# Loading sorted tokens one quad at a time into four smaller slots, in the last stage of a scan and routed-FFN kernel

## The reference

```python
x = x + _L0_attn_ref(_layernorm(x), ...)          # the scan
x = x + _L0_ffn_ref(_layernorm(x), ...)

def _L0_ffn_ref(x, weight, scale, expert_masks, router_w):
    logits = jnp.einsum('bsd,ed->bse', x, router_w)
    probs = jax.nn.softmax(logits, axis=-1)
    top1_w, top1_idx = jnp.max(probs, axis=-1), jnp.argmax(probs, axis=-1)
    w_q = jnp.clip(jnp.round(weight / THRESH), -1.0, 1.0)
    w_scaled = w_q * scale[:, None]
    def body(out, inputs):
        e_idx, mask_e = inputs
        y = jnp.einsum('bsi,oi->bso', x, w_scaled * mask_e)
        sel = (top1_idx == e_idx)[..., None]
        return jnp.where(sel, y * top1_w[..., None], out), None
```

## The time and the profile before

| | |
|---|---|
| time, median of 3 | 447.69 us (446.92 to 451.38) |
| span of the profiled execution | 460.4 us |
| last stage in it: first load issued, last output DMA begun | 389.62, 453.78 us |
| TensorE, VectorE, ScalarE, GpSimd busy | 64%, 84%, 39%, 63% |
| mean granted TensorE clock | 0.841 |

### The profile page before, as it was taken

One profiled execution on the slowest core, in us unless ns is written; L12 is line 12 of the kernel. 1 busy time (PEld: TensorE's weight loads), 2 busy tenths in 40 slices (PEclk: granted clock), 3 DMA queues, 4 the chain that ended last, 5 costly groups with the idle time before them and its releaser, 6 DMA issues.

```text
span 460.4 us, 4327 instructions
## 1 busy us (share of the span) xinstructions
PE 296.5 (64%) x1142; PEld 147.7 (32%) x1142; DVE 387.7 (84%) x400; ACT 180.5 (39%) x257; POOL 290.7 (63%) x135
## 2 busy tenths in 40 slices
PE   0868558756686675577666567476799213787780
PEld 0432222222232232222222233134376100666560
DVE  3999999999999999999999999999995970245441
ACT  1496545633464354354345335333033300322220
POOL 0645877568767767767767776776534485055554
PEclk9998777987887988978889888988978756689887
DMA  8006999920010010011010001000000334957400
GB/s 268 13 0 123 160 179 168 141 77 23 23 47 23 23 46 23 23 24 44 23 47 23 23 23 46 23 24 22 0 1 0 122 143 179 358 163 222 153 16 0
DMA packets 27902, 34.96 MB, mean 76 GB/s; under 512 B 3171, under 2 KB 22125, under 8 KB 27888
## 3 DMA queue, kind: packets, MB, share of 16 engines
q1 hardware_dynamic: 24000, 27.76, 26.1%
q0 software_dynamic: 2816, 6.32, 3.7%
q10 hardware_dynamic: 1072, 0.70, 0.6%
HBM read 20.03 MB, written 16.83 MB: 80 GB/s over the span
## 4 chain that ended last, share of the span: by engine, by line
DVE 43%; POOL 28%; PE 11%; issue 9%; DMA 3%; another core or an unknown queue 2%; ACT 1%; POOLq 0%; SPq 0%; DVEq 0%; ACTq 0%
DVE xs_sb L665 28%; POOL xs_sb L311 23%; PE bank L1063 5%; POOL sorted_tokens L355 4%; DVE bx L657 3%; PE bank L1004 2%; PE bank L1046 2%; DVE rows L632 2%; DMA x_sb<-in_L_attn_x_dram 2%; DVE st L573 1%; POOL out_dram L364 1%; DVE xn L594 1%; DVE wT L625 1%; DMA xs_sb<-sorted_tokens 1%
## 5 line engine op out<-in xcount | busy, mean ns | idle before, releaser
L311 POOL TENSOR_TENSOR xs_sb<-xs_sb,cb 128x1024 f32<-128x1024 f32 x64 | 208.0, 3270 | 84.6 <-DVE xs_sb L665 72.7
L665 DVE TENSOR_TENSOR_SCAN xs_sb<-dA,bx 128x1024 f32<-128x1024 f32 x64 | 199.8, 3160 | 0.0
L896 PE MATMUL bank<-xs_sb,cst 128*128 128x512 f32 x256 | 147.7, 706 | 2.0 <-POOL xs_sb L311 2.0
L444 ACT ACTIVATE cb<-bank 128x512 f32<-128x512 f32 x64 | 38.1, 596 | 146.8 <-POOL xs_sb L311 121.0
L860 PE MATMUL bank<-bc,pick 96*128 96x512 bf16 x64 | 22.7, 441 | 88.7 <-DVE bx L657 87.5
L657 DVE TENSOR_TENSOR bx<-bank,rows 128x1024 f32<-128x1024 f32 x64 | 74.5, 1203 | 0.1
L896 PEld LDWEIGHTS bank<-xs_sb,cst 128*128 128x128 f32 x256 | 55.0, 227 | 56.9 <-issue 51.7
L454 ACT ACTIVATE dA<-rows,a_neg 128x1024 f32<-128x1024 f32 x64 | 73.2, 1145 | 0.2
L364 POOL DMA_INDIRECT out_dram<-cb,to_token x32 | 31.8, 992 | 35.3 <-DVE cb L773 28.1
L548 ACT ACTIVATE xn<-bank 128x1024 f16<-128x1024 f16 x16 | 16.1, 1023 | 65.1 <-PE bank L1046 49.5
L860 PEld LDWEIGHTS bank<-bc,pick 96*128 (+1 forms) x64 | 4.0, 101 | 115.8 <-issue 79.5
(11 more groups left out here) (116 smaller groups left out, 295.0 us busy)
## 6 DMA issues: line engine op xcount, KB each, us to landing
sorted_tokens<-zero SPq DMA_DIRECT2D x1, 8224.0 KB, 55.4
mask_sb<-_L_ffn_expert_masks_dram SPq DMA_DIRECT2D x32, 256.0 KB, 2.7
xs_sb<-sorted_tokens SPq DMA_DIRECT2D x7, 1028.0 KB, 7.4
x_sb<-in_L_attn_x_dram SPq DMA_DIRECT2D x4, 512.0 KB, 7.8
xs_sb<-sorted_tokens SPq DMA_DIRECT2D x2, 514.0 KB, 3.7
out_dram<-cb,to_token POOLq DMA_INDIRECT x32
cst<-in_constants_dram ACTq DMA_DIRECT2D x1, 504.0 KB, 4.2
w_nat<-in_L_ffn_weight_dram SPq DMA_DIRECT2D x1, 256.0 KB, 9.1
```

The source lines that it names most:

```text
L311: pool.tensor_tensor(prod[:, j, dh, :], h[:, j, dh, :], cb[:, j, :], ALU.mult).then_inc(s_prod, 1)
L444: act.activation(cb[:, j, c * HC:(c + 1) * HC], c_ps, ACT.Copy).then_inc(s_cevac, 1)
L665: dve.tensor_tensor_scan(h[:, j, dh, :], dA[:, j, dh, :], bx[:, dh, :], 0.0, ALU.mult, ALU.add).then_inc(s_scan, 1)
L896: mm = pe.matmul(yacc[:, dh, c * HC:(c + 1) * HC], ident, prod[:, j, dh, c * HC:(c + 1) * HC], start=first, stop=last, skip_group_check=True)
```

## The change

`xs_sb` becomes the first 4112 numbers of each partition of the tile `h_and_prod` (which now has a name of its own; the trace of the changed kernel will call it so), with **four slots of one quad**. SP issues 16 loads of one quad, all alike; the load of quad `q` for `q >= 4` waits until quad `q - 4` has been transposed and finished. The first load's semaphore of its own goes. VectorE writes out four quads and then loops three times over a body of four. TensorE writes out four turns and multiplies and the turn of quad 4, loops twice over a body of four, and writes out the last four.

```diff
-        xs_sb = sb("xs_sb", [P, 4, 4, ROW])
-        h_and_prod = xs_sb[:, :, :, :].rearrange("p s t c -> p (s t c)")
+        h_and_prod = sb("h_and_prod", [P, 4 * DH * L])[:, :]
+        xs_sb = h_and_prod[:, 0:4 * 2 * ROW].rearrange("p (s t c) -> p s t c", s=4, t=2)
...
-            xs_v = xs.rearrange("(g t p) c -> g p t c", t=4, p=P)
+            xs_v = xs.rearrange("(q t p) c -> q p t c", t=2, p=P)
             sp.wait_ge(s_scat, 16 * TB)
-            for g in range(LOADS):
-                if g >= 4:
-                    sp.wait_ge(s_tps, 2 * g - 6)
-                    sp.wait_ge(s_fin, 4 * g - 12)
-                if g == 0:
-                    sp.dma_start(xs_sb[:, 0, 0:2, :], xs_v[0, :, 0:2, :]).then_inc(s_xs0, 16)
-                    sp.dma_start(xs_sb[:, 0, 2:4, :], xs_v[0, :, 2:4, :]).then_inc(s_xs[0], 16)
-                else:
-                    sp.dma_start(xs_sb[:, g % 4, :, :], xs_v[g]).then_inc(s_xs[g % 4], 16)
+            for q in range(QUADS):
+                if q >= 4:
+                    sp.wait_ge(s_tps, q - 3)
+                    sp.wait_ge(s_fin, 2 * (q - 3))
+                sp.dma_start(xs_sb[:, q % 4, :, :], xs_v[q]).then_inc(s_xs[q % 4], 16)
...
-            for s in range(8):
-                finish(s, s, 16, sent=32 if s >= 4 else None)
-            with dve.Fori(1, QUADS // 8) as i:
-                for s in range(8):
-                    finish(i * 8 + s, s, i * 16 + 16, sent=i * 64 + 32 * (s // 4))
+            for s in range(4):
+                finish(s, s, 16)
+            with dve.Fori(1, QUADS // 4) as i:
+                for s in range(4):
+                    finish(i * 4 + s, s, i * 16 + 16, sent=i * 32)
...
-            for s in range(8):
+            for s in range(4):
                 turn(s, s, 16, head=(s < 2))
                 if s:
-                    multiply(s - 1, (s - 1) % 4, experts[(s - 1) % 2], head=(s < 5))
+                    multiply(s - 1, s - 1, experts[(s - 1) % 2], head=True)
                     experts[(s - 1) % 2] = experts_of(s + 1)
-            with pe.Fori(1, QUADS // 8) as i:
-                for s in range(8):
-                    turn(i * 8 + s, s, i * 16 + 16)
-                    multiply(i * 8 + (s - 1), (s - 1) % 4, experts_of(i * 8 + (s - 1)))
-            multiply(QUADS - 1, 3, experts_of(QUADS - 1))
+            turn(4, 0, 32)
+            multiply(3, 3, experts[1], head=True)
+            with pe.Fori(1, QUADS // 4 - 1) as i:
+                for s in range(4):
+                    turn(i * 4 + (s + 1), (s + 1) % 4, i * 16 + (16 if s < 3 else 32))
+                    multiply(i * 4 + s, s, experts_of(i * 4 + s))
+            for s in range(QUADS - 4, QUADS):
+                if s < QUADS - 1:
+                    turn(s + 1, (s + 1) % 4, 16 * (QUADS // 4))
+                multiply(s, s % 4, experts_of(s))
```

More of the change, by code:

```diff
@@ L19 @@
 QUADS = TILES // 4
-LOADS = QUADS // 2
 ROW = 2 * D + 2
@@ L217, in selective_scan_then_routed_ternary_ffn @@
         s_xs = [sem(f"sorted_loaded{j}") for j in range(4)]
-        s_xs0 = sem("first_quad_loaded")
         s_tps = sem("quad_transposed")
@@ L756, in finish @@
             def finish(q, s, times, sent=None):
-                f, rows_of = s % 4, xs_sb[:, s // 2, 2 * (s % 2):2 * (s % 2) + 2, :]
+                f, rows_of = s, xs_sb[:, s, :, :]
                 here = slice(2 * f, 2 * f + 2)
-                dve.wait_ge(s_xs0 if s == 0 and sent is None else s_xs[s // 2], times)
+                dve.wait_ge(s_xs[s], times)
                 if sent is not None:
@@ L1037, in turn @@
                 j = s % 2
-                pe.wait_ge(s_xs0 if s == 0 and head else s_xs[s // 2], times)
+                pe.wait_ge(s_xs[s], times)
                 if not head:
@@ L1041, in turn @@
                 tps = bank[:, j, :].bitcast(fp16)
-                parts = xs_sb[:, s // 2, 2 * (s % 2):2 * (s % 2) + 2, 0:D].bitcast(fp16)
+                parts = xs_sb[:, s, :, 0:D].bitcast(fp16)
                 for blk in range(2):
```

## The result

The changed kernel takes 455.37 us (median of 4 runs, 454.99 to 455.89) beside 449.21 us for the kernel before (4 runs, 446.92 to 451.38). The ratio is 1.0119, with a 95% interval from 1.0061 to 1.0176. By the ratio it is slower by about 5.3 us, by the two medians by 6.2; the ratio on record is not the quotient of the medians, and I go by it. I had said 2.2 us.

A forecast was written before the change was run, and what follows sets the result against it. GpSimd's output DMAs were taken to bound the last stage; 1.0 us for late rounds of waits plus 1.2 us for load traffic gave +2.2 us on 447.69, 449.9 us (448.5 to 452; 8 in 10: 446.5 to 454.6).

The forecast's parts named there:

- What bounds the kernel before: Last stage: GpSimd's 32 output DMAs set the pace at 1.29 us each, 2.58 us a quad, beside TensorE's 2.19.
- The pauses: Four long waits between GpSimd's output DMAs in the last stage, 12.2 us in all, taken as belonging to the profiled execution.
- faster, since the pauses come from the large loads: Rival: the long output waits occur in timed runs too and vanish with the large loads; 439.1 us, chance 0.08.
- The ring of three quads: Last stage: load waits close a cycle after three quads, 7.99 us a round against GpSimd's 7.74; +1.0 us.
- Turn to multiply: Part of each round on TensorE: 0.44 us from a turn's first transpose to the first matmul behind it.
- Landing and wait for TensorE: Part of each round: 3.79 us from load issue to first transpose; 0.3 us more for output traffic, +1.2 us over four loads.
- Multiply and finish: Part of each round: 1.95 us from first matmul to VectorE's product, then 1.74 us to the second block's end.
- The signs I had named: Expected profile: TensorE waits for loads about four times, 1 to 2 us each; landings above 5 us would refute the forecast.
- First loads and SP: Start of the stage and load queue: four small first loads, and seven more DMAs of 0.36 us each; cost nothing.
- The loops: VectorE jumps back twice and TensorE once in the last stage; taken as nothing, at most 1.4 us.
- The clock rival: TensorE's clock falls to its lower level after gaps in the last stage; +4.4 us on top, 454.3 us, chance 0.17.
- The no-change rival: A round of three quads takes under GpSimd's 7.74 us, so the time stays 447.7 us; chance 0.20.

The follow-up runs named there:

- The second trace: The kernel before, run unchanged once more for another trace: 449.95 us against 450.1 us, ratio 1.0006.

## Why the prediction was right in kind and short in size

**Where the time fell.** 455.37 us lie above my range for the forecast, 448.5 to 452, and above 454.6, the top of the range of 8 in 10. Part of that is the kernel before, whose median is now 449.21, 1.5 us over the 447.69 that I reckoned from. Carried over by the ratio, 447.69 x 1.0119 = 453.0 us is within the wider range and not within the narrower. I had given 0.70 to a change of less than one per cent and 0.22 to slower by more. The ratio is on the side of the 0.22, though its interval reaches below 1.01.

**What bounds the kernel before.** Right. The second trace has 40.70 us for the output DMAs, and with half of them gone the kernel gains 10.7 us.

**The pauses.** I took 12.2 us of pauses out because the span was 12.7 us above the median, and said that they belong to the profiled execution. The number was right to take out, the reason was not: this step held by luck. Times of 461 to 462 us go with them on two chips, in every kernel with four slots or more; times of 450 us and no pauses on another. I infer that the first trace of before and the times beside it were from different conditions. That also tells why a kernel with a shorter span had a longer time. The rival "faster, since the pauses come from the large loads" falls: kernels with small loads alone have them as well.

**The ring of three quads.** Right, and it is the cause: half the output DMAs leave it bare at 2.80 us a quad, five slots remove it, three slots make it much worse. The size is where I was short. The sum had 7.99 us a round plus 0.3 for traffic, 8.29 us. Two steps from the trace of the changed kernel, the turn of quad 4 (405.91) with the multiply of quad 3, and the turn of quad 8 (417.75) with the multiply and finish of quad 7:

```profile
405.91 0.62 PE L1040 MATMUL bank<-ident,h_and_prod 128*128 128x128 f16 x8 [1.15 <-DMA h_and_prod<-sorted_tokens]
...
406.37 1.91 PE L1057 MATMUL bank<-wT,xn 128*128 x16
...
417.75 0.62 PE L1040 MATMUL bank<-ident,h_and_prod 128*128 128x128 f16 x8 [0.73 <-DMA h_and_prod<-sorted_tokens]
...
418.56 1.93 PE L1057 MATMUL bank<-wT,xn 128*128 x16 [0.19 <-issue]
...
420.53 0.69 DVE L759 TENSOR_TENSOR cb<-bank,scale_bc 128x512 f32<-128x512 f32 x1 [1.65 <-PE bank L1057]
...
421.39 0.88 DVE L767 SCALAR_TENSOR_TENSOR cb<-cb,h_and_prod 128x256 f32<-128x256 f32 x2
```

- *Turn to multiply.* I took 0.44 us from the earlier trace rows, a quad whose turn had waited for nothing. Where the expert numbers were read early it is still 406.37 - 405.91 = 0.46, though that turn had waited for its load too. In the later ones with a wait it is 418.56 - 417.75 = 0.81 us. There the load of the expert numbers stands behind the waiting turn in the program, and in the earlier trace rows it was hidden under other matmuls; put ahead of the turn, it gives 0.46 again. The part of the document on the change shows the register load behind the turn; I had read past it. The mean over quads 3 to 14 is 0.74 us, 0.30 more than in the sum. **This is a term that the sum left out.** Part of it seems to go with the loop. Inside it the distance after a wait is 0.80 to 0.84 us, in written-out code 0.61 or 0.62 (turns 14 and 15 here, 13 and 14 in the written-out kernel with four slots). The two that fit neither, 1.12 at turn 5 and 0.85 at turn 13, are those whose load of the expert numbers took 0.49 and 0.57 us rather than 0.33.
- *Landing and wait for TensorE.* Mean from issue to first transpose, over the 12 loads that waited for a slot: 4.39 us, from 3.93 to 5.21. I had 3.79 + 0.3 = 4.09, so 0.30 short. The landings themselves are 3.9 to 5.2 us, median 4.3; in two of the twelve, quads 7 and 10, TensorE was still at the multiply before when the load was there. The loads are issued 2.2 to 3.7 us apart (401.98, 404.42, 406.62, 410.14) and take longer than that, so they overlap each other beside the output traffic. My landing without traffic came from one small load, and what traffic costs from the quickest large one.
- *Multiply and finish.* 420.53 - 418.56 = 1.97 and 421.39 + 0.88 - 420.53 = 1.74, against 1.95 and 1.74 in the sum. Right.

The sum of these means is 0.08 + 4.39 + 0.74 + 1.98 + 1.75 = 8.94 us a round, 0.65 more than mine; over four rounds 2.6 us. That makes 2.2 + 2.6 = 4.8 us, and the traces show 44.94 - 40.70 = 4.2 us between the output DMAs. The four rounds of the forecast can also be read directly: quads 0, 3, 6, 9 and 12 are finished at 401.90, 410.06, 418.80, 427.81 and 437.20 us. That is 35.3 us, 8.8 a round, and 4.3 us above 4 x 7.74. The timed difference of 5.3 us has an interval of 2.7 to 7.9 us, which holds all of these and lies above the 2.2 us of the forecast. What the timed difference has beyond the stage's 4.2 us no run explains; the interval is wide enough for it to be nothing.

**The signs I had named.** I expected TensorE to wait about four times for 1 to 2 us, at quads 7, 10 and 13. It waits nine times after the first, for 0.2 to 1.15 us, and not at quads 7 and 10. Three chains of loads run side by side, three quads apart, and TensorE takes the quads in their order, so a late quad holds up the other chains too. The chain that ended last in this trace goes through the loads of quads 5, 9, 12 and 15. Landings above 5 us were to prove me wrong: one of the twelve took 5.2.

**The other terms.** First loads and SP at nothing: not contradicted, and the ring accounts for the stage within 0.6 us. The loops at nothing: no idle time of 1 us at a jump, but about 0.2 us of the distance from turn to multiply seems to go with them. What they cost in time was never measured by itself where it would have shown, since the four-slot kernels that were to tell it had pauses. That stays open.

**The clock rival.** It fell in this kernel. TensorE waits up to 1.15 us for a load and is busy 5.75 to 7.26 us of 8, and from 402 us on the granted clock stays at 1.00, 2.4 GHz, against the 0.50 of the earlier trace rows:

```profile
402.00:410.00 8.00, 5.75 (x63) 4.66 (x60) 5.02 (x15) 2.52 (x3) 6.09 (x6) 1.00 0.76 233
410.00:418.00 8.00, 7.01 (x69) 5.67 (x70) 4.42 (x15) 2.60 (x3) 4.92 (x5) 1.00 0.74 223
...
434.00:442.00 8.00, 7.26 (x70) 5.79 (x69) 4.54 (x14) 2.36 (x3) 5.46 (x6) 1.00 0.35 106
```

With three slots, where TensorE waits 3.0 to 3.6 us for a load at seven turns, it came true in part of the rounds. The no-change rival fell where the stage has no pauses and was the outcome on the two chips with them, but not for its reason (a ring under GpSimd's pace). The pauses give some 10.9 us for three quads there, more than the ring's 8.9, and I take it that the ring is hidden in that; no run shows it by itself.

**What stays open** is where the pauses come from. They come 10.7 to 11.0 us apart, three quads, in the first trace of the kernel before and in every trace with four slots or more on the two chips. With three slots on one of these chips no such wait without a named engine is seen, and TensorE is less dense there. VectorE stands 3.3 to 5.7 us in each, ScalarE for about as long or in two parts. TensorE does not stop as a whole, as I had read it from the earlier trace rows; in that same pause it goes on by single matmuls:

```profile
419.48 0.27 PE L1063 MATMUL bank<-wT,xn 128*128 x1 [0.59 <-issue]
...
420.21 0.22 PE L1046 MATMUL bank<-ident,xs_sb 128*128 128x128 f16 x1 [0.40 <-issue]
```

No run tells more.

## What to carry to other kernels

Count how many steps a ring of buffers really holds: with four slots, and a consumer that takes step q + 1 before it finishes q, it is three, and a round of the ring has everything in it, landing, issue, register loads and both engines. When a wait becomes exposed, price what stands behind the waiting instruction in the sequencer anew; a row in which it was hidden shows its duration, not its place. And where span and time disagree, run the kernel before again before reading anything from the trace.

## What the runs showed of the hardware

- The same program took 450 us on one chip and 462 to 463 us on two others, and a change worth 1.2% where it took 449 us was worth nothing on those two (ratios 0.9999 and 0.9974).
- Time was 1.8 to 1.9 us above the span in every execution for which both are on record, as 455.69 and 453.9, 448.32 and 446.5.
- Taking out 16 of 32 output DMAs of 1.29 us saved 10.7 us by the medians. The two traces differ by 9.1 us (spans 446.5 and 437.4): 7.6 us between the first and the last DMA (40.70 and 33.09), the missing last one included, 1.4 us behind the start of the last one, and 0.1 ahead of the first. The other 1.6 us lie between those executions and the medians.
